# A hand-kept order table of a five-engine transformer and state-space kernel, replaced by another order of the same steps

## What is computed

```python
mod = (silu(c) @ wmod).reshape(32, 6, 1, 256); sa, ca, ga, sb, cb, gb = ...
h = layernorm(x) * (1 + ca) + sa
# --- first half: attention and a selective scan side by side, then a feed-forward layer
xn = ln(h); q, k, v = xn @ q_w, xn @ k_w, xn @ v_w          # 16 heads of 16
attn = softmax(causal(q k^T / 4)) @ v @ o_w
x_ssm, z = split(xn @ in_proj_w)                             # 512 channels each
x_c = silu(causal_conv4(x_ssm)); dt, B, C = x_c @ x_proj_w ...; dt = softplus(dt @ dt_w + dt_b)
h_t = exp(dt * A) * h_{t-1} + (x_c * dt) * B_t ;  y_t = sum_n C_t h_t   # 512 channels x 16 states
ssm = ((y + x_c * D) * silu(z)) @ ssm_out_w
x1 = h + alpha * attn + (1 - alpha) * ssm
x = x + ga * (x1 + gelu(ln(x1) @ w1) @ w2)
# --- second half: a linear layer with eight routed low-rank experts (top 2 of 8)
h = layernorm(x) * (1 + cb) + sb
x = x + gb * (h @ base_w^T + 2 * sum_e p_e (h A_e) B_e)
```

## Time and profile before

| | |
|---|---|
| median of three runs | 6004.91 us |
| the profiled execution | 6000.29 us, of which the span from first to last instruction is 5998.3 us |
| PE | 5304.5 us busy, 88% of the span |
| DVE | 5134.6 us, 86% |
| POOL | 4334.4 us, 72% |
| ACT | 4065.3 us, 68% |
| PE's granted clock, mean | 0.958 |
| HBM traffic | 134 GB/s over the span |

### The profile page before, as it was taken

The page is one execution under the profiler, slowest core; times in us unless marked ns, Lnnn a source line. Parts: engine busy times, 40 slices in busy tenths (PEclk is TensorE's granted clock), DMA queues, the critical chain, the costliest instruction groups (busy, mean ns, idle before and its releaser), DMA issues.

```text
span 5998.3 us, 116936 instructions
## 1 busy us (share of the span) xinstructions
PE 5304.5 (88%) x32280; PEld 3529.3 (59%) x32280; DVE 5134.6 (86%) x7776; ACT 4065.3 (68%) x6407; POOL 4334.4 (72%) x3569
## 2 busy tenths in 40 slices
...
GB/s 131 126 140 142 139 140 161 132 126 139 137 146 149 117 145 122 143 161 129 141 127 140 140 161 129 128 139 138 145 156 111 150 126 151 147 140 127 152 118 41
DMA packets 521729, 814.77 MB, mean 136 GB/s; under 512 B 80432, under 2 KB 227288, under 8 KB 520976
## 3 DMA queue, kind: packets, MB, share of 16 engines
...
HBM read 716.50 MB, written 88.38 MB: 134 GB/s over the span
## 4 chain that ended last, share of the span: by engine, by line
PE 43%; DVE 19%; issue 18%; ACT 9%; POOL 7%; DMA 3%; SPq 1%; ACTq 1%; DVEq 1%; POOLq 0%
PE pM L1090 8%; PE pY L939 5%; DVE pD L1200 5%; PE pM L1081 5%; DVE mx L1258 4%; POOL state L584 3%; PE pM L948 3%; PE pM L1070 2%; PE pM L1014 2%; PE pM L1027 2%; DVE state L1208 2%; ACT pD L707 2%; PE pM L1119 2%; DVE xc L1240 2%; DMA region<-mrow 2%
## 5 line engine op out<-in xcount | busy, mean ns | idle before, releaser
L584 POOL TENSOR_TENSOR state<-scan_in,bc 128x512 f32<-128x512 f32 x2048 | 2559.1, 1273 | 488.3 <-PE pY L939 405.5
L1200 DVE TENSOR_TENSOR_SCAN pD<-pD,state 128x512 f32<-128x512 f32 x1536 | 1853.8, 1218 | 174.6 <-ACT pD L707 159.0
L707 ACT ACTIVATE pD<-scan_in,A 128x512 f32<-128x512 f32 x2048 | 1389.7, 691 | 629.7 <-DVE state L1208 510.7
L939 PE MATMUL pY<-ident,state 128*128 128x128 f32 x8192 | 1225.6, 283 | 13.2 <-POOL state L571 8.0
L939 PEld LDWEIGHTS pY<-ident,state 128*128 128x128 f32 x8192 | 941.8, 146 | 272.4 <-issue 157.2
L1208 DVE TENSOR_TENSOR state<-pD,bc 128x512 f32<-128x512 f32 x1536 | 1020.4, 682 | 24.7 <-DMA bc<-bc_d 3.2
L1258 DVE TENSOR_REDUCE mx<-pM 128x1 f32<-128x512 f32 (+3 forms) x1408 | 855.9, 630 | 65.9 <-PE pM L1029 64.8
L571 POOL TENSOR_TENSOR state<-state,bc 128x512 f32<-128x512 f32 x512 | 646.9, 1272 | 336.3 <-DVE state L1200 306.8
L808 ACT ACTIVATE region<-pM 128x512 f32<-128x512 f32 (+1 forms) x1408 | 726.1, 559 | 201.7 <-PE pM L1047 178.9
L1045 PE MATMUL pM<-region 98*128 98x512 bf16 (+3 forms) x2048 | 527.8, 310 | 220.9 <-DMA region<-mrow 89.1
L1200 DVE TENSOR_TENSOR_SCAN state<-pD,state 128x512 f32<-128x512 f32 x512 | 615.2, 1214 | 90.4 <-issue 48.9
...
## 6 DMA issues: line engine op xcount, KB each, us to landing
bc<-bc_d SPq DMA_DIRECT2D x2048, 256.0 KB, 4.1
region<-qk_d SPq DMA_DIRECT2D x640, 128.0 KB, 3.6
...
region<-qk_d SPq DMA_DIRECT2D x256, 64.0 KB, 2.9
...
```

What stands on the lines that cost most here:

```text
L584: nc.gpsimd.tensor_tensor(state[:, e % RING], us[:, parity(b), k // N * JP + e % JP, :], bc[:, k % BC_SLOTS, 0, :], ALU.mult).then_inc(b_o ...
L707: act.activation(pD[DECAY_BANK[e]][:], dts[:, parity(b), j], ACT.Exp, scale=A[:, j, n:n + 1]).then_inc(a_ok.sem, 1)
L939: ins = pe.matmul(y_part(t, e % JP), state[:, e % RING, t * P:(t + 1) * P], ident[:], is_transpose=True, start=False, stop=(e % PASS >= PA ...
L1200: v.tensor_tensor_scan(h if e in POOL_C else decay, decay, h, 0.0, ALU.mult, ALU.add)\
```

## The change

Only the two tables change: the order of steps in `ORDER` for all five engines, and the banks in `PLACE`. The sets of steps are the same on each engine, with the same instructions; no wait rule, buffer or size is touched. Most steps move by one to four places. The tables also begin at another place of the cycle: ACT's at `ud` (before: `-yt2`), DVE's at `+l0s` (before: `scan14`), PE's at `mx1_0` (before: `-f2_0`), POOL's at `fill19` (before: `-f1_0`), SP's at `-rc21` (before: `-rb27`). Two lines of each kind from the diff:

```diff
     "POOL": """
-        -f1_0 +l0s fill20 fill21 +l0a +l0b fill22 fill23 +l0c fill24 +l1s fill25 fill26 fill27 pc22 pc23 -x2 -x2b
-        fill28 -l3s +ql0 fill29 -xb +ql1 fill30 +ql2 fill31 fill32 fill33 pc30 pc31 fill34 fill35 +ql3 -gb fill36
+        fill19 fill20 +l0s fill21 +l0a fill22 +l0b fill23 fill24 +l1s +l0c fill25 pc22 fill26 pc23 fill27 -x2
+        -x2b -l3s +ql0 fill28 fill29 -xb +ql1 fill30 +ql2 fill31 fill32 fill33 pc30 pc31 +ql3 fill34 fill35
...
 PLACE.update((name, 0) for name in """
-    xt0 qk1 v1 mx0_2 mx0_3 mx0_4 mx0_7 z3 st0_0_0 mx1_2 st0_1_0 st0_2_0 st0_3_0 mx1_6 mx1_7 mx1_10 mt1 mx2_0
+    qk0 qk1 z0 mx0_2 mx0_3 mx0_4 mx0_6 mx0_7 z3 mx1_1 st0_0_3 mx1_3 st0_1_3 st0_2_0 st0_3_0 mx1_4 mx1_6
```

More of the change, by code:

```diff
@@ L1363 @@
     "SP": """
[L1364 to L1367, removed]
+        -rc21 -rb22 -rc19 -rb24 -ld3 -rb25 -rb23 -rc22 -mt2 -rc25 -rc23 -rb26 -rb27 -rc26 -rc24 xp -rb28 ld0
@@ L1376 @@
+        +pc14 +pc15
     """,
     "ACT": """
[L1378 to L1387, removed]
@@ L1388 @@
-        yt0 ot1 yt1 +dec4 +v1
+        ud v0 dec2 v1 dec3 -ot0 -yt0 -ot1 -yt1 dec4 -yt2 -yt3 dec5 dec6 dec7 dec8 z0 dec9 dec10 dec11 dec12 z1
+        dec13 -l2a dec14 -h2t0 -h2t1 dec15 dec16 z2 dec17 -f1_0 -f1_1 -f1_2 dec18 dec19 -f1_3 -f1_4 dec20 +l0a
+        dec21 -f1_5 -f1_6 dec22 -f1_7 -gelu dec23 mt0 dec24 z3 dec25 +l1a +xt0 dec26 dec27 zsilu dec28 st0_0_0
+        st0_0_1 +xt1 st0_0_2 st0_0_3 dec29 st0_1_0 +qk0 +qm0 st0_1_1 -l3a st0_1_2 +qk1 -h3t0 -h3t1 +qm1 +qk2 +xs0
+        +qm2 dec30 dec31 +xs1 +qk3 st0_1_3 dec32 st0_2_0 st0_2_2 +qm3 -route2 st0_3_0 -axt dec33 dec34 -out0
@@ L1389 @@
+        +dec0 +dec1
     """,
     "PE": """
[L1391 to L1395 removed]
@@ L1401 @@
-        st3_3_0 add60 add61 pv3_2 pv3_3 on3 +v1 ot0 add62 add63 ot1 yt0 yt1 +skip0 +add0 yt2 +add1 +z0 +add2 yt3
-        +add3 +mx0_1 +add4 sso0 sso1 +add5 +add6 +add7 +add8 +mx0_2 +z1 +z2 +add9 +add10 +mx0_3 h2t0 h2t1 +add11
-        +add12 +mx0_4 +add13 f1_0 f1_1 f1_2 f1_3 f1_4 +mx0_5 f1_5 f1_6 f1_7 +add14 +mx0_6 +add15 +add16 +mx0_7
-        +mx0_8 +mx0_9 +mx0_10 +add17 +z3 +add18 +mt0 +mx1_0 +add19
+        mx1_0 -f2_0 +xt0 -f2_1 st0_0_0 st0_0_1 mx1_1 st0_0_2 add20 +xt1 st0_0_3 add21 st0_1_0 +qk0 add22 add23
```

79 lines of the change are left out of this document (47 added, 32 removed).

## The result

| | before | after |
|---|---|---|
| median of the runs | 6002.6 us (4 runs) | 6051.88 us (4 runs, 6045.14 to 6053.41) |
| ratio | | 1.0081, 95% interval 1.0062 to 1.0099 |
| profiled execution, span | 6000.29, 5998.3 us | 6049.22, 6047.2 us |
| PE's granted clock, mean | 0.958 | 0.959 |

The change makes the kernel slower by 0.8%, 49 us. Forecast were 6040 us and a range of 5968 to 6082 us, with a chance of 0.61 for slower. The sign and the range held. The terms of the sum did not all hold, as the traces show.

What follows compares the result with a forecast made beforehand. PE was taken as full from `yt0` to `f2_1`, DVE nearly full behind it, with jumps back in line. 1.1 us by 31 distances (34.1) plus jumps 2.6 make 36.7 us: 6040 us forecast, range 5968 to 6082.

Steps and rivals of the forecast that it cites:

- The term for each batch: Sum of `fill28`, around `mt2` and softplus: 1.1 + 0.2 - 0.2 = 1.1 us, by 31 distances 34.1 us.
- The jumps: ACT, DVE and PE jumping back to their table starts: three holes stay in line, +0.2 us for each of 13 long distances.
- `fill28`: `fill28` behind `ql0` on POOL makes DVE wait 2.4 us ahead of `scan28`; 1.1 us per batch taken, bounds 0 and 2.4.
- what gives some of it back: DVE, late from the `fill28` wait, no longer waits as long at `qk1`, `qk2` and `xs1`: 1.45 us returned.
- `lora`: PE's `lora` group comes behind a score group and two additions, so DVE's last `lora` instruction waits another 0.2 us.
- Around `mt2`: PE idles in one piece of about 3.9 us, against DVE's vanishing waits: +0.2 us, bounds -1.0 and +1.7.
- The third rival: Much slower: the single 3.9 us idle time at `mt2` keeps PE's clock low 3.4 us more per batch; 6087 us, chance 0.13.
- Softplus: `c56` right behind `scan56` gets `dec58` out of ACT's way before `sp2`: 0.2 us gained, between 0 and 0.85.
- PE's full stretch: From `yt0` to `f2_1` PE holds the same steps and takes the same time: 0, with 0.5 us either way.
- SP's table: Rows wait for later slots; POOL late by up to 1 us for `fill58`, hidden by its 5.90 us wait ahead of `u0`.
- The second rival: Faster: jumps of ACT and DVE fall into slack, hiding one 3.5 us hole per long distance; 5944 or 5961 us, chance 0.25.

Runs made afterwards that it cites:

- e3: The kernel before, with only the loop heads of ACT, DVE and PE where the changed kernel has them: 5983.85 us, ratio 0.9959.
- e4: The changed kernel with the loop heads of ACT, DVE and PE put back to their old places: 6060.54 us, ratio 1.0079 to the kernel before.
- e1: The changed kernel with `fill28` put back ahead of `l3s` in POOL's order: 6047.87 us, ratio 1.0062 to the kernel before.
- e2: The kernel before, with only `fill28` moved behind `ql0` in POOL's order: 6145.66 us, ratio 1.0237.
- e6: The changed kernel with `st0_3_0`, `add26` and `add27` moved back behind `lora` on PE: 6053.09 us, ratio 1.0067 to the kernel before.
- e12: The changed kernel with the order from `f2_0` to `mt1` and its PSUM banks as before, on PE, DVE, ACT and POOL: 6021.02 us, ratio 1.0029.
- e9: The changed kernel with e6's PE order, `scan35` and `c35` ahead of `mt1` on DVE, `dec35` and `ql3` moved to suit: 6109.29 us, ratio 1.0172.
- e7: The changed kernel with SP's table alone as in the kernel before: 6052.74 us, ratio 1.0068 to the kernel before.

## Why the prediction was right, and which of its steps were not

- **Distances, time.** Forecast 36.7 us, measured 49. The sum came near because two errors of opposite sign met. The term for each batch, forecast 1.1 us, was 2.3 (18 short distances), over 31 distances 72 us instead of 34.1. The jumps, forecast +2.6 us, were 13 x (0.11 - 2.33) = -29 us, by the distances of the trace; e3 has such a gain on the old order (25 us), e4 could not show it on the new one. The rest is the start and the end, +8.6 and -3.2 us, which the prediction counted as unchanged. That the number came near is luck in this sense.
- **`fill28`.** The wait was sized right (2.14 for 2.4 us), its price was not. It is about 0.4 us per batch, if anything (11 us by 31, e1), since without `mx1_4` and `c28` ahead of it `qk1` would have waited as long. The failed step is "what gives some of it back": it counted the waits of the old order and not those that the new order has without `fill28`. The bounds of 0 and 2.4 us held for this kernel; in the old order the price is 4.6 us (e2), outside them.
- **`lora`.** Forecast +0.2 us, measured 1.28 us in the row. Taken away, it brought nothing (e6), so its size was wrong and it was not the cause.
- **Between `lora` and `mt2`** the prediction had no term, and 1.6 us of the 2.3 arise there; 0.5 are there at `lora`, 0.2 come behind `mt2` (means of 18). It took DVE's full stretch as one piece and asked only for new waits. It should have asked what DVE does ahead of `mt1`, where PE sets the time: a step that slips behind `mt1` adds its whole length to DVE's full stretch (35 instructions instead of 33). e12 shows that the order up to `mt1` makes about half of it, by the start of `mt2`. That `scan35` and `c35` alone make it is a reading of the traces: moving them without the rest of that order (e9) made other waits.
- **Around `mt2`.** Forecast +0.2; from `mt2` to `xp` the lateness goes from 2.1 to 2.0 us. PE's idle time ahead of the third group's scores did grow, to 3.1 us from 2.6 (forecast 3.9), but the mean clock in the ten microseconds behind was 0.74, against 0.71 before. The third rival did not happen here; e9 shows its mechanism at `mt1`.
- **Softplus** was to give 0.2 us and gave nothing: the wait ahead of `sp3` is 1.23 us instead of 0.85. The medians have 0.4 us lost there (`sp3` +2.6, `scan0` +3.0) and 0.5 at `mt3`, the means of 18 have +2.2 at `sp3` and +2.3 at `scan0`. Not taken apart.
- **PE's full stretch**: 0 with 0.5 either way; +3.0 at `yt0`, +3.2 at `x2` (means: +2.2 and +2.3). Right.
- **SP's table**: cost 0, right (e7), though POOL's waits for rows grew by 237 us, far more than the 1 us for `fill58` that it named.
- **The jumps**: forecast three holes of the same lengths in line. They were 7.3 us instead of 10.0, and the new places are worth 1.8 us for each long distance in the old order (e3). The second rival's mechanism, jumps that cost less at the new places, happened, short of its point of 2.6 us.
